# Two of four decays written to SBUF ahead of each silu, and a re-ordered DMA queue, in a Mamba and mixture-of-experts kernel

## The reference

```python
# layer 1: a selective state space block
h = x * rsqrt(mean(x*x) + eps) * norm_scale
xs, res = split(h @ w_in)                         # 512 channels each
res = silu(res)
xs = silu(causal_depthwise_conv(xs) + conv_b)
delta, B, C = split(xs @ w_xproj)                 # 16 states
delta = softplus(delta @ w_dt + b_dt)
deltaA = exp(delta * A)                           # the decay
deltaBx = (delta * xs) * B
state[t] = deltaA[t] * state[t-1] + deltaBx[t]    # the scan
y = sum_n state * C
x = layernorm(x + x + ((y + xs * D) * res) @ w_out)
# layer 2: shared expert and 8 routed experts, the best 2 of 8 per token
n = x * rsqrt(mean(x*x) + eps) * norm_weight
shared = relu(n @ sw1 + sb1) @ sw2 + sb2
routed = sum over the 2 chosen experts of w_e * (relu(n @ ew1[e] + eb1[e]) @ ew2[e] + eb2[e])
x = layernorm(x + shared + routed)
```

## Time and profile before

| | us |
|---|---|
| median of 3 runs | 1727.56 (1727.55 to 1731.47) |
| the profiled execution | 1725.55 |
| its span | 1723.5 |
| busy share of the span: PE, DVE, ACT, POOL | 86%, 69%, 53%, 55% |
| row load of stage 3, issue to landing, median | 2.1 |
| stage 1, first scan to last | about 68 to 1058 |
| stage 3, first transpose to last product | about 1133 to 1670 |

### The profile page before, as it was taken

How to read it: one execution, slowest core, us unless ns; L and a number is a source line. 1 busy time by engine, 2 the same in 40 slices (tenths; PEclk the granted TensorE clock), 3 DMA queues, 4 the chain that set the end, 5 groups by cost and what they waited for, 6 DMA issues and landing times.

```text
span 1723.5 us, 24541 instructions
## 1 busy us (share of the span) xinstructions
PE 1483.5 (86%) x6945; PEld 967.7 (56%) x6946; DVE 1193.8 (69%) x2113; ACT 906.6 (53%) x1778; POOL 952.4 (55%) x590
## 2 busy tenths in 40 slices
PE   7386799989989989989988769967999999999970
PEld 3131235525525525526535326767999999999960
DVE  4499999999999999999999997212333333333327
ACT  4477666777766777665786553212333333333324
POOL 1677797798798798788799884301111111111115
PEclk9697998998998998988999889888999999999995
DMA  5833653455554444534535521936555555555538
GB/s 157 220 94 86 147 135 92 119 131 123 124 127 113 124 120 123 138 96 123 135 94 131 139 67 63 302 103 237 182 179 179 180 179 178 180 180 183 181 126 264
DMA packets 136951, 252.14 MB, mean 146 GB/s; under 512 B 15313, under 2 KB 68418, under 8 KB 136754
## 3 DMA queue, kind: packets, MB, share of 16 engines
q1 hardware_dynamic: 130402, 233.49, 48.6%
q0 software_dynamic: 6480, 17.83, 2.8%
HBM read 205.76 MB, written 45.51 MB: 146 GB/s over the span
## 4 chain that ended last, share of the span: by engine, by line
PE 51%; DVE 26%; ACT 11%; issue 7%; SPq 3%; DMA 2%; POOL 0%; DVEq 0%; ACTq 0%; POOLq 0%
DVE psH L1124 16%; PE psH L1541 15%; PE psP L1552 14%; PE psP L1382 6%; DVE big L1133 6%; PE psP L1371 4%; ACT psH L960 2%; PE psA L1480 2%; PE psA L1461 2%; PE psP L1400 2%; PE psP L1445 2%; SPq L710 1%; PE psA L1471 1%; PE psP L1529 1%; DMA ew_s<-in_L_ffn_ew_dram 1%
## 5 line engine op out<-in xcount | busy, mean ns | idle before, releaser
L472 POOL TENSOR_TENSOR big<-big,B 128x2048 f32<-128x2048 f32 x128 | 578.1, 4530 | 106.1 <-PE psA L1480 51.0
L960 ACT ACTIVATE psH<-big,A_q 128x512 f32<-128x512 f32 x512 | 351.7, 691 | 146.0 <-DVE big L1133 121.5
L1133 DVE TENSOR_TENSOR big<-psH,C 128x512 f32<-128x512 f32 x512 | 350.8, 685 | 0.0
L1124 DVE TENSOR_TENSOR_SCAN psH<-psH,big 128x512 f32<-128x512 f32 x256 | 313.3, 1224 | 50.9 <-ACT psH L960 31.1
L576 POOL DMA_INDIRECT con_dram<-eo,dest x71 | 68.3, 962 | 490.8 <-ACT eo L1032 482.9
L1124 DVE TENSOR_TENSOR_SCAN psH<-psH,carry,big 128x512 f32<-128x512 f32 x256 | 331.8, 1296 | 11.0 <-ACT psH L960 11.0
L1541 PE MATMUL psH<-nTb,ew_s 128*128 128x128 f32 x2272 | 271.4, 279 | 12.9 <-DMA ew_s<-in_L_ffn_ew_dram 8.8
L1541 PEld LDWEIGHTS psH<-nTb,ew_s 128*128 128x128 f32 x2272 | 270.8, 196 | 17.1 <-issue 13.7
L1552 PE MATMUL psP<-big,hT 128*128 x1136 | 257.0, 379 | 0.7 <-DVE eb L1290 0.7
L1480 PE MATMUL psA<-big,gsum 128*32 128x512 f32 x1024 | 218.3, 661 | 44.5 <-DVE big L1133 43.4
L1261 DVE TENSOR_TENSOR hT<-psH,vecs 128x512 f32<-128x512 f32 x142 | 98.2, 692 | 196.4 <-PE psH L1541 196.4
(11 more groups left out here) (173 smaller groups left out, 1544.4 us busy)
## 6 DMA issues: line engine op xcount, KB each, us to landing
ew_s<-in_L_ffn_ew_dram SPq DMA_DIRECT2D x71, 1024.0 KB, 4.8
big<-ud_dram SPq DMA_DIRECT2D x128, 512.0 KB, 8.6
ud_dram<-ud SPq DMA_DIRECT2D x32, 512.0 KB
xb<-rows_dram SPq DMA_DIRECT2D x71, 130.0 KB, 2.1
B<-bc_dram SPq DMA_DIRECT2D x128, 64.0 KB, 5.7
C<-bc_dram SPq DMA_DIRECT2D x128, 64.0 KB, 5.6
big<-in_L_ffn_ew_dram SPq DMA_DIRECT2D x8, 1024.0 KB
big<-con_dram SPq DMA_DIRECT2D x16, 512.0 KB, 8.8
```

The lines of the kernel that those rows point to most:

```text
L472: nc.gpsimd.tensor_tensor(X[:, Q % NX], rep[:, g % 2, 1], B4[:, f:f + 1, :].broadcast_to([P, NR, TC]), ALU.mult).then_inc(bx_ready, 1)
L960: nc.scalar.activation(psH[:, r, :], rep[:, g % 2, 0, r, :], ACT.Exp, scale=A_q[:, c, r, f:f + 1]).then_inc(dA_ready, 1)
L1124: nc.vector.tensor_tensor_scan(psH[:, r, :], psH[:, r, :], X[:, Q % NX, r, :], start, ALU.mult, ALU.add).then_inc(scan_done, 1)
L1133: nc.vector.tensor_tensor(X[:, Q % NX, r, :], psH[:, r, :], C4[:, f, :], ALU.mult).then_inc(hc_ready, 1)
```

## The change

It does two things.

1. At q = 3 and q = 8, the steps with a silu, the decays of r = 2 and 3 (`ahead`) do not go to `psH`. ScalarE writes them to SBUF, to halves of `xr` at q = 3 and of `spe` at q = 8 (`decay_of`), right after the decay of r = 1, ahead of the silu, without waiting for VectorE. The scans of those two parts then read the decay from there and still write `psH`. Where the tile is even, the copies of the last column stay necessary; the one of r = 3 stands behind the silu, and the scan now waits for its `carry`. As `xr` is now used at q = 3, `load_xr` waits for that scan, and stands behind `load_rep(k, 2)`.
2. In the SP queue, `store_acc(NT - 1, 0)` goes ahead of the zeroing loop, `load_up(2, 0)` ahead of the fourth `load_block`, and the load of `xall` is cut into 32 DMAs of 128 KB, one per pass of the loop over blocks.

```diff
+        AHEAD = (3, 8)
+        def ahead(q, r):
+            return q in AHEAD and r >= 2
+        def decay_of(q, r):
+            if not ahead(q, r):
+                return psH[:, r, :]
+            if q == 8:
+                return spe[:, r - 2]
+            return xr[:, 2 * (r - 2):2 * (r - 1), :].rearrange("p s d -> p (s d)")
...
             def load_xr(k):
                 pwait(sp, k - 1, ("T", DC - 1))
+                if k >= 2:
+                    sp.wait_ge(scan_done, ((k - 2) * NQ + 3) * NR + NR)
                 sp.dma_start(xr[:], rows_of(k)).then_inc(xr_here, 16)
...
-                if k + 2 < NT:
-                    load_xr(k + 2)
                 store_ud(k, 2)
                 if k >= 2:
                     store_acc(k - 2, 1)
                 load_rep(k, 2)
+                if k + 2 < NT:
+                    load_xr(k + 2)
                 store_ud(k, 3)
...
             for i in range(2):
                 load_up(i, i)
+            store_acc(NT - 1, 0)
             with sp.Fori(0, E) as e:
...
-            for h in range(2):
-                store_acc(NT - 1, h)
+            store_acc(NT - 1, 1)
             for i in range(2):
                 sp.wait_ge(T_done, i + 1)
                 sp.wait_ge(meta_done, i + 1)
                 load_block(i + 2, i)
-            load_up(2, 0)
+                if i == 0:
+                    load_up(2, 0)
...
             sp.wait_ge(acc_out, 16 * 2 * NT)
-            sp.dma_start(xall[:], acc_dram.rearrange("(t p) d -> p t d", p=P)).then_inc(x_back, 16)
+            acc_rows = acc_dram.rearrange("(t p) d -> p t d", p=P)
             with sp.Fori(1, NBLK // 2 - 2) as t:
                 one_pass(t)
+                sp.dma_start(xall[:, ds(t - 1, 1)], acc_rows[:, ds(t - 1, 1)]).then_inc(x_back, 16)
...
-                if Q:
-                    act.wait_ge(hc_ready, products(Q - 1, r))
-                keep_state(Q - 1, r)
-                nc.scalar.activation(psH[:, r, :], rep[:, g % 2, 0, r, :], ACT.Exp,
+                if not ahead(q, r):
+                    if Q:
+                        act.wait_ge(hc_ready, products(Q - 1, r))
+                    keep_state(Q - 1, r)
+                elif q == 8 and r == 2:
+                    act.wait_ge(u_ready, (k + 1) * CH)
+                nc.scalar.activation(decay_of(q, r), rep[:, g % 2, 0, r, :], ACT.Exp,
                                      scale=A_q[:, c, r, f:f + 1]).then_inc(dA_ready, 1)
...
-                        decay(k, q, r)
+                        if not ahead(q, r):
+                            decay(k, q, r)
+                        if q in AHEAD and r == 1:
+                            for later in range(2, NR):
+                                decay(k, q, later)
+                            act.wait_ge(hc_ready, products(k * NQ + q - 1, 2))
+                            keep_state(k * NQ + q - 1, 2)
                         parts(k, (q, r))
+                        if q in AHEAD and r == 1:
+                            act.wait_ge(hc_ready, products(k * NQ + q - 1, 3))
+                            keep_state(k * NQ + q - 1, 3)
...
+                if ahead(q, r) and k % HALVES == 0:
+                    dve.wait_ge(carry_done, (k // HALVES) * NQ * NR + (q - 1) * NR + r + 1)
                 start = carry[:, q, r:r + 1] if k % HALVES else 0.0
-                nc.vector.tensor_tensor_scan(psH[:, r, :], psH[:, r, :], X[:, Q % NX, r, :], start,
+                nc.vector.tensor_tensor_scan(psH[:, r, :], decay_of(q, r), X[:, Q % NX, r, :], start,
                                              ALU.mult, ALU.add).then_inc(scan_done, 1)
```

More of the change, by code:

```diff
@@ L756, in _ @@
             sp.wait_ge(acc_out, 16 * 2 * NT)
-            sp.dma_start(xall[:], acc_dram.rearrange("(t p) d -> p t d", p=P)).then_inc(x_back, 16)
+            acc_rows = acc_dram.rearrange("(t p) d -> p t d", p=P)
+            assert NBLK // 2 - 2 == NSUBS + 1
             with sp.Fori(1, NBLK // 2 - 2) as t:
                 one_pass(t)
+                sp.dma_start(xall[:, ds(t - 1, 1)], acc_rows[:, ds(t - 1, 1)]).then_inc(x_back, 16)
             load_up(NBLK - 2, 1)
@@ L1320, in moments4 @@
                 if k == 0:
-                    dve.wait_ge(x_back, 16)
+                    dve.wait_ge(x_back, 16 * NSUBS)
                 dve.wait_ge(both_ready, k + 1)
```

## The result

The changed kernel takes **1784.95 us** (median of 4 runs, 1783.87 to 1786.02), beside 1727.97 (4 runs, 1727.55 to 1731.47) for the kernel before: ratio **1.0325 [1.0307, 1.0343]**. It is 3.3% slower. The forecast was 1772 in a range of 1736 to 1796: sign and range hold, and the time came out 13 us above the forecast, on the number of rival C.

A forecast was written before the change was run, and what follows sets the result against it. The prediction took VectorE to bound stage 1, with GpSimd nearly as full, and TensorE stage 3. Stage 1 +62 and stages 2 and 3 -18 made +44 us on 1725.55, or 1772 us as a median; range 1736 to 1796.

The forecast's parts named there:

- rival C: GpSimd keeps its hold over back-to-back multiplications; a waiting scan enters only when it pauses; 13 us more, 1785 us; chance 0.12.
- That a scan is blocked as an element-wise instruction is: Stage 1: scans with two SBUF inputs wait for a running GpSimd instruction that reads SBUF; placed sum 67 us.
- Rival A: Scans from SBUF are not blocked, so the silus' 11 and the later stages' 18 us come in; 1698.5 us; chance 0.13.
- Rival B: Fewer scans meet a multiplication, so half of the added waits in stage 1 stay; 1738 us; chance 0.17.
- How long the r = 2 scan waits at q = 8: Tile 4: it waits to the multiplication border at 638.2, then r = 3 waits to 643.9, 8.1 us later than before.
- The near ties at q = 3 of even tiles: Three later even tiles: a scan coming first loses some 3.3 us less; half of that counted, -5 us.
- q = 3 of odd tiles: Tile 5: the r = 3 scan at 721.42 meets a multiplication running to 725.0; 3.6 us.
- The silus: Stage 1, q = 3 and 8: early decays shrink the stalls behind the silus, a gain of 11 us without blocking.
- Stage 1 in all: All tiles: blocked scans' waits, with the silu gain inside and the near ties taken off, add 62 us.
- the placing: Stage 1: new scans set on GpSimd's old timeline, tile by tile, to find their waits; sum 67 us.
- Stage 2 and 3: After the scans: queue changes remove TensorE's waits and slow up parts; together -18 us, independent of stage 1.
- the early store: `store_acc(7, 0)` ahead of the zeroing loop lets the first transpose start earlier: -0.7 us, between -2 and +1.5.

The follow-up runs named there:

- with a pause: Changed kernel, but at q = 10 and 11 GpSimd waits for its previous multiplication to complete before issuing the next; 1775.88 us, ratio 1.0308.
- with pieces: Changed kernel, but GpSimd's multiplications at q = 5, 9, 10 and 11 are each cut into four of 512 elements; 1778.74 us, ratio 1.0321.
- run with fills: Changed kernel, but GpSimd's multiplications at q = 4, 5, 9, 10 and 11 are replaced by a memset of X; 1700.01 us, ratio 0.9875.
- fastest kernel: Changed kernel, but only r = 2 decays go ahead: to idle PSUM at q = 8 and, in tiles 0 and 1, q = 3; else xr; 1693.87 us, 0.9828.
- queue alone: Changed kernel with no decay ahead of the silu, only the SP queue changes kept; 1705.57 us, ratio 0.9897.

## Why the prediction was right, and where it was off

**That a scan is blocked as an element-wise instruction is: right.** This was the choice that gave the sign, drawn from one wait of 2.28 us of L1335. The scans with `xr` and `spe` average 4.2 us. Rival A is out, by the changed kernel and by the run with the decays in SBUF at their old place. Rival B is out too: at q = 3 and q = 8 all later tiles lose.

**How long the r = 2 scan waits at q = 8: the step that failed, in size.** "It waits to 638.2" put the scan's entry at the next border between two multiplications, and then made r = 3 wait for the third. In tiles 0 and 1 the scans do get in at the border, and these tiles came out as placed (6.0 and 10.9 us, placed at 5 and 11). In tiles 2 to 7 r = 2 waits for the whole run, 9.97 us in tile 4 and 9.20 in tile 5, and r = 3 is free. That is rival C's mechanism, which had 0.12 and was priced at 13 us more. Measured, the q = 8 part of a tile adds 5.9 to 6.1 us in the even tiles 2, 4 and 6 and 6.4 in tiles 3 and 5, where the forecast had 4.9 and 5.1: 1.0 to 1.3 more each. The runs with a pause and with pieces show both sides of it. The Trainium skill's rule ("SBUF — State Buffer", "Who interferes with whom") says that the second to issue blocks until the first is finished. The blocking agrees with the trace. Its length, read of a single instruction, agrees in tiles 0 and 1 (3.45 us, to the border) and not in tiles 2 to 7: what had to finish there was all that GpSimd ran without a pause, up to nine pieces (11.03 us).

**The near ties at q = 3 of even tiles: -5 us, not earned.** In tile 4 scan and multiplication started in the same hundredth of a microsecond, 634.40, and the scan lost; tiles 2 and 6 add 3.2 and 3.1 us there too. In tile 2 the scan had even started first, by 0.15 us by these rows (VectorE, then GpSimd), and by 0.14 in the runs with a pause and with pieces:

```profile
363.93 5.77 DVE L1157 TENSOR_TENSOR_SCAN psH<-xr,big 128x512 f32<-128x512 f32 x1
```

```profile
364.08 4.51 POOL L486 TENSOR_TENSOR big<-big,B 128x2048 f32<-128x2048 f32 x1
```

The multiplication kept its 4.51 us and the scan waited it out. So "if it comes first, the tile loses some 3.3 us less" doesn't hold for a lead as small as this.

**q = 3 of odd tiles: +3.6 forecast, +4.25 measured** in tiles 3 and 5. The forecast saw what a scan suffers from a multiplication, and not that the r = 2 scan, itself two-input, delays the scatter ahead of it by 0.9 us.

**The silus: 11 us.** They can't be read from the changed kernel, where blocking covers them. The run with fills shows them, with the same decays ahead but a faster GpSimd: against the kernel before, q = 3 is 1.31 us shorter in tiles 2, 4 and 6, and q = 8 is 1.06 to 1.08 us shorter in the four even tiles and 1.54 to 1.56 in tiles 1, 3 and 5. That is 2.4 us in an even tile (forecast 1.6 to 1.8) and 1.6 in an odd one (1.43), 12.9 in all without q = 3 of tile 0. The fastest kernel gains 0.7% over the queue alone, 12 us, with r = 2 alone ahead: a figure of that size, for another version of the idea.

**Stage 1 in all: +62 forecast, +77 to 79 measured.** By tile, from the first scans of steps in both traces, 6.0, 10.9, 14.3, 9.9, 7.4, 9.9, 9.5 and 11.1 us; the placing had 5, 11, 8.4, 8.7, 8.1, 8.7, 8.1 and 9.5. What is left of tile 2's excess is a single thing at its start, worth 4.7 us: TensorE runs there at a mean granted clock of 0.74, where the same place before had 0.93 (stretches of 26 us; busy time of each engine and its instructions, then the clock, the DMA share and GB/s; before first, then after).

```profile
307.00:333.00 26.00, 24.12 (x110) 15.52 (x110) 24.61 (x30) 17.88 (x37) 16.80 (x9) 0.93 0.60 132
```

```profile
324.00:350.00 26.00, 24.20 (x84) 14.05 (x85) 20.36 (x24) 13.18 (x28) 15.41 (x9) 0.74 0.54 112
...
327.68 3.68 PE L1494 MATMUL psA<-sw_s,hT 128*128 128x256 f32 x8
340.23 3.78 PE L1494 MATMUL psA<-sw_s,hT 128*128 128x256 f32 x8
```

Eight matmuls of the shared expert take 1.89 us at the upper level (2.4 GHz) and 3.78 at the lower (1.2); before, these two groups took 1.99 and 2.79. ScalarE waits for them, and VectorE for its decays: 0.69, 2.19, 0.90 and 1.86 us, against 1.15 and 0.24 before. TensorE was busy 8.19 of the 10 us before the fall, and 8.09 before the stretch that kept its clock. From tile 2 on about one slow group a tile is common to all kernels here, the one before included (3.78 us at 445.04, say); two in a row are not. They stand in tile 2 of the changed kernel, and at the start of tile 4 in the run with pieces (3.58 and 3.78 us at 586.25 and 598.71) and in the run with fills (3.58 and 3.78 us at 561.27 and 573.73), with 3.07 us lost at q = 0 each time, as in tile 2 here (3.08). The runs with late decays and with a pause have held-up scans too and no such pair. So the pair isn't tied to the held-up scans; what sets its place stays open.

**Stage 2 and 3: -18 us forecast, -18.8 measured** (0.5 + 18.3). Terms: the early store -0.5 against -0.7, the two stalls of stage 3 -18.3 against -17.5. In the trace of the queue alone the second is nearly the same, -17.8, but the first is not: from SP's load to the first transpose it has 60.9 us, 4.4 less than before. There the zeroing loop begins 44.2 us after the load, as before (44.3); in the changed kernel it begins after 48.2. So the agreement of the first term is in part luck. `load_xr` at nothing: the wait for decays hardly changes with it (43.9 us against 42.1), nor does a new one stand beside it; but stage 1 of the queue alone is 3.3 us longer, so nothing below that size is shown.

**A count that was wrong:** "some 20 of up to 5.7 us" for GpSimd's multiplications. Five take 5.42 to 5.44 us, all in tiles 0 and 1, and those 0.9 us each are the whole 4.5 us by which the 128 grew. In the later tiles, where a scan is let in only at a pause, it delays no multiplication by more than 0.1 us; it delays a scatter.

So 13 us of 57 were missing. The whole-run wait gives some 7.5 of them (1.0 to 1.3 in each of five tiles, and tile 7 as a whole 1.6 above its placing), the ties 5, the pair of slow groups 4.7 and the scatters of tiles 3 and 5 1.3; smaller differences of the other sign take some back. That the time lies on rival C's 1785 is luck: C's mechanism held in six tiles of eight and was worth about half of its 13 us.

## What to carry to other kernels

Before a tensor is moved from PSUM to an idle SBUF buffer, count the SBUF inputs of each VectorE instruction that reads it: from one to two, beside a GpSimd that is nearly always busy, turned 1.2 us into 4.2 on average, and cost over 70 us (1.0325 against 0.9897). With an idle PSUM bank for 10 of 16 such decays, those of r = 2 alone, the idea gained some 12 us (0.9828); with r = 3 ahead in PSUM too it was not tried. And where one engine waits for another's instruction, ask how many stand behind it without a pause.

## What was not expected of the hardware

- In tiles 2 to 7 VectorE's two-input scan got in only when GpSimd paused: with its own 1.1 us it took 9.97 us across the last two of three multiplications back to back, 11.03 across the last nine of twelve pieces, and 4.96 where a semaphore wait stood between the multiplications. In tiles 0 and 1 it got in at the next border without a pause (3.45 us, and 1.43 between pieces). The cause of the difference is open.
- A scan that started 0.15 us ahead of a multiplication was held up by it all the same (5.77 us).
- A GpSimd fill doesn't hold the scan up, as was expected (1.28 us inside a single fill of 1.80).
- A row scatter of GpSimd's is held up by such a scan (1.86 us instead of 0.98), but doesn't hold it up (1.23 us beside one).
